# Layer two's channel sums: float32 squares as one operand, or as two bf16 parts with the low part made by GpSimd

## The reference

```python
x = x + _L0_conv_ref(_gn(x), ...)   # shifted-window attention, 7x7 windows, 12 heads of 8
x = x + _L1_conv_ref(_gn(x))        # below; _gn is a group norm over 3 channels and all places
...
w0, w1, w2 = 1, 5, 20
s = box_sum(box_sum(x, 1, w0), 2, w1)
num = box_sum(s * s, 3, w2)
d = box_sum(box_sum(box_sum(x * x, 1, w0), 2, w1), 3, w2)
denum = d * norm[None, :, :, None]
return jnp.nan_to_num(num / denum, nan=FILL)
```

## Time and profile before

| | |
|---|---|
| Median of 3 runs | 3241.63 us (3240.45 to 3242.56) |
| Profiled execution, span | 3240.4 us; the page gives no other time for it |
| TensorE matmuls busy | 3157.0 us, 97% |
| VectorE busy | 2883.8 us, 89% |
| ScalarE busy | 2282.5 us, 70% |
| GpSimd busy | 2267.1 us, 70% |

### The profile page before, as it was taken

The page is one execution under the profiler, slowest core; times in us unless marked ns, Lnnn a source line. Parts: engine busy times, 40 slices in busy tenths (PEclk is TensorE's granted clock), DMA queues, the critical chain, the costliest instruction groups (busy, mean ns, idle before and its releaser), DMA issues.

```text
span 3240.4 us, 146752 instructions
## 1 busy us (share of the span) xinstructions
PE 3157.0 (97%) x60544; PEld 2668.2 (82%) x60544; DVE 2883.8 (89%) x4882; ACT 2282.5 (70%) x4705; POOL 2267.1 (70%) x2522
## 2 busy tenths in 40 slices
PE   4999999999999999999999999999999999999997
PEld 3888888888888888888888888888888888888885
DVE  5999999999999999999999999999999999999983
ACT  2577777777777777777777777777777777777764
POOL 4677777777777777777777777777777777767763
PEclk8999999999999999999999999999999999999995
DMA  3333333333333333333333333333333333333320
GB/s 85 93 84 94 86 89 90 91 87 90 91 87 89 95 85 87 93 89 87 95 86 87 94 88 88 88 92 87 90 93 85 88 95 86 88 97 75 77 65 24
DMA packets 385696, 280.19 MB, mean 86 GB/s; under 512 B 261931, under 2 KB 384908, under 8 KB 385036
## 3 DMA queue, kind: packets, MB, share of 16 engines
q1 hardware_dynamic: 384652, 270.69, 33.9%
q10 hardware_dynamic: 384, 0.11, 0.0%
HBM read 39.35 MB, written 38.54 MB: 24 GB/s over the span
## 4 chain that ended last, share of the span: by engine, by line
PE 92%; ACT 3%; SPq 2%; issue 1%; DVE 1%; DMA 0%; ACTq 0%; POOL 0%; DVEq 0%; POOLq 0%
PE pP L472 22%; PE pO L487 19%; PE pS L460 9%; PE pM L555 6%; PE pM L572 5%; PE pM L510 5%; PE pM L442 5%; PE pM L561 5%; PE pM L394 3%; PE pM L500 3%; PE pM L400 3%; PE pM L401 3%; PE pM L402 3%; PE pM L581 2%; SPq L335 1%
## 5 line engine op out<-in xcount | busy, mean ns | idle before, releaser
L1050 POOL TENSOR_TENSOR T<-T,MX 128x588 f32<-128x588 f32 x1024 | 1212.3, 1185 | 889.8 <-DVE MX L827 886.8
L662 ACT ACTIVATE P<-pP 128x588 f32<-128x588 f32 x1024 | 673.7, 658 | 418.4 <-PE pP L472 411.9
L820 DVE TENSOR_TENSOR T<-pS,table 128x588 f32<-128x588 f32 x1024 | 783.5, 765 | 82.4 <-PE pS L460 53.8
L472 PE MATMUL pP<-K,T 113*128 113x113 f32 x6144 | 818.9, 269 | 0.8 <-ACT P L662 0.8
L827 DVE TENSOR_REDUCE MX<-T 128x12 f32<-128x588 f32 x1024 | 778.3, 760 | 25.9
L487 PEld LDWEIGHTS pO<-V,P 128*49 128x49 f32 x24576 | 646.2, 125 | 162.4 <-ACT P L662 69.2
L487 PE MATMUL pO<-V,P 128*49 128x18 f32 x24576 | 747.1, 200 | 0.4 <-DVE O L857 0.4
L472 PEld LDWEIGHTS pP<-K,T 113*128 113x128 f32 x6144 | 602.6, 141 | 93.3 <-issue 1.0
L460 PE MATMUL pS<-KE,QS 128*64 128x196 bf16 (+1 forms) x8192 | 466.4, 231 | 17.3 <-DMA KE<-KS 16.3
L767 ACT ACTIVATE rd<-pM,tiny 112x384 f32<-112x384 f32 x224 | 130.3, 582 | 362.1 <-PE pM L561 362.0
L460 PEld LDWEIGHTS pS<-KE,QS 128*64 128x64 bf16 x8192 | 309.8, 110 | 18.6 <-DMA KE<-KS 17.0
(11 more groups left out here) (94 smaller groups left out, 5976.6 us busy)
## 6 DMA issues: line engine op xcount, KB each, us to landing
KE<-KS SPq DMA_DIRECT2D x512, 147.0 KB
KS<-knh SPq DMA_DIRECT2D x768, 49.0 KB
QS<-qnh SPq DMA_DIRECT2D x768, 49.0 KB
out<-tok_out SPq DMA_DIRECT2D x384, 84.0 KB
tok_in<-x SPq DMA_DIRECT2D x224, 84.0 KB
KS<-knl SPq DMA_DIRECT2D x384, 49.0 KB
QS<-qnl SPq DMA_DIRECT2D x384, 49.0 KB
tok_in<-x SPq DMA_DIRECT2D x224, 63.0 KB
```

The source lines that it names most:

```text
L472: mm = pe.transpose(pP[:, c, QN * at:QN * at + QN], T[j % 4][0:QN, 2 * h:2 * h + 2, :], pick)
L662: act.activation(P32[j % 3][:, :, :].rearrange("p (c a w) q -> p c a (w q)", c=2, w=2), src, ACT.Exp).then_inc(p_made, 1)
L820: dve.tensor_tensor(T[j % 4][:, :, 0:L].rearrange("p (b h) k -> p b h k", b=2), pS[:, :, 0:HALF].rearrange("p b (h k) -> p b h k", k=L), t ...
L1050: pool.tensor_tensor(t, t, MX[j % 4][:, :].unsqueeze(2).broadcast_to([128, HEADS, L]), ALU.subtract).then_inc(shifted, 1)
```

## The change

The squares are given to TensorE as two bf16 numbers. The high one is not made at all: it is the upper half of each float32 word, read in place with a step of two bf16 elements (`SQ_high`, `ybox2_high`). The low one is the float32 less that half, in bf16 (`SQ_low`, `ybox2_low`), and GpSimd subtracts it. The band, which is zeros and ones, gets a bf16 copy. Each float32 matmul becomes two bf16 ones that add up in PSUM, and the loaded operand is 128 columns wide in place of 112. TensorE waits for the low parts.

```diff
-Y_AT, PAIR_AT, FOUR_AT, BOX_AT, BOX_SQ_AT = 44, 44, 45, 46, 50
-SQ_AT, DEEP_AT, WIDE_AT, RATIO_AT, OUT_AT, STORE_AT = 47, 50, 51, 52, 53, 54
+Y_AT, PAIR_AT, FOUR_AT, BOX_AT, BOX_SQ_AT, LOW_BOX_AT = 44, 44, 45, 46, 49, 50
+SQ_AT, LOW_SQ_AT, DEEP_AT, WIDE_AT, RATIO_AT, OUT_AT, STORE_AT = 46, 47, 50, 51, 52, 53, 54
...
+        ybox2_high, SQ_high = (t[:, :].bitcast(BF16).rearrange("c (t half) -> c t half", half=2)[:, :, 1]
+                               for t in (ybox2, SQ))
+        band16 = sb("band16", [C, C], BF16)
...
             def deep_squares(G):
...
-                pe.wait_ge(sq_made, G + 1)
+                pe.wait_ge(sq_low_made, G + 1)
...
                 for t in range(TILES):
-                    mm = pe.matmul(bankB[0:ROWS2, C * t:C * t + C], SQ[:, ROWS2 * t:ROWS2 * t + ROWS2], band,
-                                   start=True, stop=True)
+                    at = ROWS2 * t
+                    pe.matmul(bankB[:, C * t:C * t + C], SQ_high[:, at:at + 128], band16[:, :], start=True, stop=False)
+                    mm = pe.matmul(bankB[:, C * t:C * t + C], SQ_low[:, at:at + 128], band16[:, :],
+                                   start=False, stop=True)
                 mm.then_inc(csq_made, 1)
...
             def deep_y(G):
...
-                pe.wait_ge(ybox2_made, G + 1)
+                pe.wait_ge(ybox2_low_made, G + 1)
...
+            def low_squares(G):
+                pool.wait_ge(sq_made, G + 1)
+                if G:
+                    pool.wait_ge(csq_made, G)
+                pool.tensor_tensor(SQ_low[:, 0:GTOK], SQ[:, 0:GTOK], SQ_high[:, 0:GTOK], ALU.subtract
+                                   ).then_inc(sq_low_made, 1)
+
+            def low_box(G):
+                pool.wait_ge(ybox2_made, G + 1)
+                if G:
+                    pool.wait_ge(num_made, G)
+                pool.tensor_tensor(ybox2_low[:, 0:GTOK], ybox2[:, 0:GTOK], ybox2_high[:, 0:GTOK], ALU.subtract
+                                   ).then_inc(ybox2_low_made, 1)
...
-            zero = [*tok_in, P32[0], XL, V[0], V[1], T[0], T[1], T[2], T[3], O[0], O[1], Y]
+            zero = [*tok_in, P32[0], XL, V[0], V[1], T[0], T[1], T[2], T[3], O[0], O[1], Y,
+                    SQ, ybox2, SQ_low, ybox2_low]
...
                 for j in steps(s + 1):
                     shift(j)
+                for G in groups(s, LOW_SQ_AT):
+                    low_squares(G)
+                for G in groups(s, LOW_BOX_AT):
+                    low_box(G)
```

More of the change, by code:

```diff
@@ L184, in build @@
         ybox = sb("ybox", [C, GTOK])
-        ybox2 = sb("ybox2", [C, GTOK])
-        SQ = sb("SQ", [C, GTOK])
+        ybox2 = sb("ybox2", [C, GTOK + 16])
+        SQ = sb("SQ", [C, GTOK + 16])
+        ybox2_low = sb("ybox2_low", [C, GTOK + 16], BF16)
+        SQ_low = sb("SQ_low", [C, GTOK + 16], BF16)
+        ybox2_high, SQ_high = (t[:, :].bitcast(BF16).rearrange("c (t half) -> c t half", half=2)[:, :, 1]
+                               for t in (ybox2, SQ))
+        band16 = sb("band16", [C, C], BF16)
         csq = sb("csq", [ROWS2, TILES * C])
@@ L253, in build @@
         sq_made = signal("sq_made")
+        sq_low_made = signal("sq_low_made")
+        ybox2_low_made = signal("ybox2_low_made")
         y_made = signal("y_made")
@@ L546, in deep_squares @@
                 k = STEPS * (G // GROUPS) // 4 + G % GROUPS + DEEP_AT // 4
-                pe.wait_ge(sq_made, G + 1)
+                if G == 0:
+                    pe.wait_ge(dve_setup, 8)
+                pe.wait_ge(sq_low_made, G + 1)
                 if k + QK_AHEAD < ALL_UNITS:
@@ L571, in deep_y @@
                 for t in range(TILES):
-                    mm = pe.matmul(bankC[0:ROWS2, C * t:C * t + C], ybox2[:, ROWS2 * t:ROWS2 * t + ROWS2], band,
-                                   start=True, stop=True)
+                    at = ROWS2 * t
+                    pe.matmul(bankC[:, C * t:C * t + C], ybox2_high[:, at:at + 128], band16[:, :],
+                              start=True, stop=False)
+                    mm = pe.matmul(bankC[:, C * t:C * t + C], ybox2_low[:, at:at + 128], band16[:, :],
+                                   start=False, stop=True)
                 mm.then_inc(num_made, 1)
@@ L745, in square @@
                     act.wait_ge(csq_made, G)
-                act.activation(SQ[:, :], X1[m % 2][:, GTOK * v:GTOK * v + GTOK], ACT.Square,
+                act.activation(SQ[:, 0:GTOK], X1[m % 2][:, GTOK * v:GTOK * v + GTOK], ACT.Square,
                                bias=g[1][:, NB:NB + 1], scale=g[1][:, RS:RS + 1]).then_inc(sq_made, 1)
@@ L752, in square_box @@
                     act.wait_ge(num_made, G)
-                act.activation(ybox2[:, :], ybox[:, :], ACT.Square).then_inc(ybox2_made, 1)
+                act.activation(ybox2[:, 0:GTOK], ybox[:, :], ACT.Square).then_inc(ybox2_made, 1)
             def keep_squares(G):
@@ L929, in make_tables @@
                 dve.wait_ge(bias_in, 16 * L)
-                setup_link(8, dve.tensor_copy(table[0][:, :].rearrange("p (h k) -> p h k", h=HEADS),
+                setup_link(9, dve.tensor_copy(table[0][:, :].rearrange("p (h k) -> p h k", h=HEADS),
                                               bias_raw[:, :, :].rearrange("p k h -> p h k")))
@@ L933, in make_tables @@
                     mask = K[:, K_MASK + L * t:K_MASK + L * t + L].unsqueeze(1).broadcast_to([128, HEADS, L])
-                    setup_link(9 + i, dve.tensor_tensor(
+                    setup_link(10 + i, dve.tensor_tensor(
                         table[t][:, :].rearrange("p (h k) -> p h k", h=HEADS),
@@ L955, in _ @@
             setup_link(7, dve.tensor_copy(DG[C:C + 1, :], K[C:C + 1, K_ID:K_ID + C + 1]))
+            setup_link(8, dve.tensor_copy(band16[:, :], band))
             for s in range(FIRST_SLOT, END_SLOT + 1):
```

## The result

The changed kernel takes 3695.9 us (median of 4 runs, 3664.8 to 3711.4) against 3241.4 us for the kernel before (median of 4): the ratio is 1.139, 95% interval 1.136 to 1.142. I had forecast 3446 us and a range to 3550. The sign and the place were right; the size was too small by 250 us.

What follows compares the result with a forecast made beforehand. TensorE bounds the kernel before; after the change a circle of waits through GpSimd's `low_box` sets the pace. 31 images x 6.90, -10 for the drain, +1 for the rest: +205 us on 3241.6, 3446 us, range 3370 to 3550.

Steps and rivals of the forecast that it cites:

- TensorE is the bound, `deep_y` gets the wait, `low_box` stands right in front of it: TensorE's `deep_y` waits for GpSimd's `low_box`, queued behind a shift: stall 1.63 us, +0.93 us for an ordinary group.
- The circle of 13.24 us: Loop from `deep_y` through scores, VectorE, GpSimd's shifts and `low_box` back to `deep_y`: 13.24 us a unit against 12.32.
- the wake: Delay from the end of `low_box` to TensorE's start of `deep_y`: 0.15 us, bounds 0.05 and 0.30.
- An image: One image's groups, most of them delayed at `deep_y`, sum to +6.90 us; one image at some 104.6 us.
- The drain: Last image, at 1.2 GHz with no shifts ahead of `low_box`: both sums gain, some -10 us for seven groups.
- The load of 128 columns: Eight bf16 matmuls of a sum on TensorE: 0.42 us taken, bounds 0.34 (stream alone) and 0.77 (nothing gained).
- The rest: ScalarE's moved squares and `low_squares` cost nothing; extra fills and a small copy at the start, 1 us.
- Ours stays above the first: TensorE, busy 88%, stays above a drain window with 3.95 us busy in 5 that kept the full clock.
- the second rival: The clock falls as well: 2.5 us more in 217 units, near 3990 us; chance 4%.
- my signs of being wrong: Low parts far under 1 us, the shift ahead of `low_box` earlier against TensorE, or a falling clock.
- The range: 3370 to 3550 us for the kernel's time, keeping the likeliest case and leaving the rest out.
- the case that I took for likeliest: The circle through `low_box` sets the pace as computed: 3446 us, own range 3379 to 3550, chance 83%.

Runs made afterwards that it cites:

- e3: The changed kernel with `low_box` ahead of its slot's shift on GpSimd, not behind it: 3212.0 us, ratio 0.991.
- e7: The changed kernel with `low_box`'s subtraction done twice on GpSimd, the second waiting for the first: 4143.6 us, ratio 1.281.
- e5: The changed kernel with `low_box` one slot earlier on GpSimd (LOW_BOX_AT 49, not 50): 3112.5 us, ratio 0.961.
- e6: As e5, but with 112 loaded columns in place of 128: 3128.3 us, ratio 0.966.
- e1: The changed kernel with seven useless bf16 matmuls on TensorE ahead of `deep_y`'s wait: 3459.9 us, ratio 1.067.
- e8: As e7, with twelve filling matmuls on TensorE ahead of `deep_y`'s wait: 3681.7 us, ratio 1.136.

## Why the prediction was wrong, point by point

- *TensorE is the bound, `deep_y` gets the wait, `low_box` stands right in front of it.* Right: 201 waits of 1.6 us, "near 1.6 us, about 200 times". An ordinary unit's stall is 1.5 us, not 1.63.
- *The circle of 13.24 us.* Right: 13.13, and e3, shorter by one shift, and e7, longer by one subtraction, land on 11.99 and 14.13. But the 0.11 us are smaller than the errors of the terms. `low_box` took 0.93 us in place of 1.06, its lower bound; the eight matmuls 0.35 in place of 0.42; the wake 0.06 in place of 0.15: 0.29 less. Against that stands a reading of mine. The chain gives `deep_y` and what follows it as starting when the piece before ends; TensorE's timeline of before has the same matmuls 0.16 us sooner:

```profile
1613.91 0.94 PE L572 MATMUL pM<-K,ybox 96*112 96x96 f32 x8
1614.68 0.55 PE L500 MATMUL pM<-K,O 113*96 113x113 f32 x4
```

  I took the start of TensorE's stretch from the chain and its neighbours from timelines. From `L500` on to GpSimd's first shift, 6.33 us in the sum, the changed kernel takes 6.51 (1867.07 to 1873.58). Part of the closeness is luck.
- *An image.* The intervals that kept the full clock add up to 104.3 us against the forecast 104.6. Here too two errors cancel in part: four ordinary units grow by 0.80 us each where I had 0.93, and the rest of the image, with its sixth and seventh group and the unit without one, by 3.4 us where I had 3.2.
- *The drain.* I expected it to give back 9 us with the start. In e3 the images account for 26 of the 29 us that the kernel is faster, so start and drain together gave back about 3. No run takes the drain by itself.
- *The load of 128 columns.* I took a price of my own, 0.42 us for eight, over the rule of the Trainium skill ("TensorE: Matmul & The Clock Gate", section "Weight-path perf modes"), that 128 columns not in float32 load faster. The rule holds here: 0.34 us in e5, 0.35 in the changed kernel, is what the stream alone takes (the lower bound of the prediction), and e6, with 112 columns and 0.41 us, shows that it is the number of columns.
- *The rest* (ScalarE's moves, `low_squares`, the fills) at nothing or 1 us: no wait of size for them in the profile after.
- *The clock.* **This step failed.** The prediction put it as "Ours stays above the first" and gave the rival 4%. The step that failed is the comparison behind it: it set the busy share over a whole unit, 88%, against one window of the drain that had 79% and kept its clock. A share over 13 us says nothing of a stall inside it: the windows around 1808 have 0.85 busy of 3.00. What I called the second rival is the case that came, in part of the units: 64 falls, 498 us at half clock, where the sum had nothing. e1 and e8 put the price of it at 236 and 462 us by taking it away, with all waits of the circle in place. Of that rival's size, 2.5 us lost in every unit, I had too much: 236 us over 217 units are 1.1 us each (and 5 us of work at half clock, as it says, would lose 5 us; 2.5 is what 5 us of time loses). Of its chance I had far too little, though a falling clock was among my signs of being wrong.
- *The range* ended at 3550 because it left that case out. With e1's 3460 the case that I took for likeliest would have been hit to 14 us.

## What to carry to other kernels

When a change adds a wait, look up what stands ahead of the awaited instruction on its engine at that moment, and close the circle: the sum of its parts is the pace, however idle each engine looks on average. Then ask what the stall does to TensorE's clock. Here a stall of 1.5 us in each round, on a TensorE that had not paused before, lost more through the clock (236 us) than through the longer rounds (218 us in e1), and filling it with useless matmuls is a quick test of that. The cure here was to move the awaited work by one slot, not to drop the change.

## What the hardware showed unexpectedly

- TensorE's clock fell from 2.4 to 1.2 GHz after single stalls of 1.5 to 2.3 us between stretches of solid work (64 of 170 of them), in a kernel where it was 88% busy; after stalls under 1.2 us in none of 396, all kernels of the table together (drain and start left out). It stayed low for 3.4 to 20 us.
- A bf16 load of 128 columns, read with a step of two, hides under a stream of 96 columns (0.043 us a matmul in e5), while one of 112 columns does not (0.051 us in e6).
- GpSimd's subtraction of 448 elements with a strided bf16 operand took 931 ns, the same as that of 392 elements with both bf16 operands contiguous.
